# A scan layer on one core: the seam between the power levels and the state inputs reordered

## The chip, the cores and the metric

The kernel runs on one core of one Trainium2 chip. The metric is the device time of one execution in microseconds (us). Five engines run side by side, each with its own instruction queue, and order each other by semaphores: TensorE (PE), VectorE (DVE), ScalarE (ACT), GpSimd (POOL) and SyncE (SP), which issues most of the DMA transfers.

## The reference, cut to what matters

Input x is (1, 8192, 512) in f32. It is normalised and modulated, goes through a linear state-space layer with a dense 16x16 matrix A per channel, and then through a layer norm, a GELU, an output product and a small feed-forward block. The part around the change is the state-space layer:

```python
def step(h, x_t):
    h = jnp.einsum('dnm,bdm->bdn', A, h) + Bm[None] * x_t[..., None]
    y_t = jnp.einsum('dn,bdn->bd', Cm, h) + Dm * x_t
    return (h, y_t)
_, y = jax.lax.scan(step, h0, jnp.swapaxes(x, 0, 1))
```

## The kernel before, in words

Time is cut into 64 chunks of 128 steps (NC = 64, L = 128). Within a chunk the layer is a convolution with the taps C A^k B; between chunks a state of 16 numbers per channel is carried. The 512 channels are done in two halves of 32 groups of 8 channels (8 x 16 = 128 partitions). For each half the engines go through these stages:

- **Levels** (L1198, L1201): 28 steps (STEPS = 7 levels x OCT = 4 octets of 8 groups) double the number of known vectors A^k B (array PV) and of transposed ones (WP). In each step POOL lays out the power of A as block diagonals (L421), DVE transposes them (L847), PE multiplies, and ACT copies the results from PSUM (L638 to L640, semaphore lvl_ev). Step n of PE waits for the transposes of step n and for the copies of step n - 2. In half 0, ACT also normalises the columns of x between the steps (L579, semaphore xh_r), and DVE takes their statistics.
- **Column sums** (L905): when the last level of an octet is copied, DVE sums PV over time, one reduction for each of four octets. L942 makes from them the bias SB of the state inputs (sb_r).
- **Taps** (L1211): 64 matmuls of CM (C spread over groups, made by POOL at L454, cm_r) with PV give the convolution taps (semaphore k_mm). DVE takes them from PSUM (L951 to L956), and SP writes them to memory, from where they are later loaded as Toeplitz tiles.
- **State inputs**: for q = 0 to 7, PE transposes four groups of PV (L1220, `input_mats(q)`, ut_mm), ACT copies them to SBUF (L648, ut_ev), PE multiplies them with x (L1237, the input product, u_mm), ACT scales and biases the even channels and writes them into PV (L567, `even_inputs`), and DVE adds the odd ones (L967, u_ev). Product q waits for u_ev of q - 4.
- **Scan** (L1262) over the chunks, and then the **output products** (L1305, L1310) for 32 groups.

After both halves comes the feed-forward part, from 368 us to the end. Every engine's order is written out by hand in its queue; each instruction waits on semaphores, and whatever stands behind a waiting instruction on the same engine waits too. Two queues matter here. In DVE's, the reduction of octet o stood right behind the transposes (L847) of a step and ahead of those of the next step, in each of the last three steps. In PE's, the 64 tap matmuls stood behind the last level step and ahead of the first input transposes.

Of the kernel before, what the change touches and what calls it, by code (L numbers as in the profile page):

```python
# [12 lines left out]
P = 128  # L13
# [3 lines left out]
L = P  # L17
# [6 lines left out]
OCT = HG // 8  # L24
# [5 lines left out]
STEPS = LEVELS * OCT  # L30
SSTEPS = SCANS * OCT
HSTEPS = STEPS + SSTEPS
ESTEPS = HSTEPS - OCT
# [40 lines left out]
def adaln_ssm_kernel(nc, x_in, A_in, Bm_in, Cm_in, Dm_in, lnw_in, lnb_in, Wo_in, bo_in,  # L74
# [12 lines left out]
    with ctx:  # L87
# [55 lines left out]
        CM = UR.rearrange("p (g c) -> p g c", c=4 * GC)  # L143
# [407 lines left out]
        def _(act):  # L551
# [7 lines left out]
            def even_inputs(half, q):  # L559

                act.wait_ge(S["parca_r"], 2)
                act.wait_ge(S["sb_r"], half + 1)
                act.wait_ge(S["u_mm"], 8 * half + q + 1)
                ps = PS[:, q % 4, :].rearrange("p (g c a) -> p g a c", g=4, a=2)
                for i in range(4):
                    g = half * HG + 4 * q + i
                    ins = act.activation(PV[:, 4 * q + i, H0:H0 + NC], ps[:, i, 0, :], ACT.Identity, scale=parca[:, 0, g:g + 1],  # L567
                                         bias=SB[:, g:g + 1])
                ins.then_inc(S["ua_r"], 1)
# [196 lines left out]
        def _(dve):  # L766
# [134 lines left out]
            def column_sums(half, o):  # L901

                dve.wait_ge(S["lvl_ev"], half * ESTEPS + STEPS - OCT + o + 1)
                sums = SB[:, half * HG + 8 * o:half * HG + 8 * o + 8]
                dve.reduce_sum(sums, PV[:, 8 * o:8 * o + 8, 0:L], AX.X).then_inc(S["sums_r"], 1)  # L905

            for half in range(HALVES):
                base = half * HSTEPS
                for n in range(STEPS):
                    if half == 0 or n >= AHEAD:  # L910
                        power_mats(half, n)
                    if half == 0 and n == 0:
                        first_column(0)
                    if half == 0 and n == 6:
                        first_tap()
                    if half == 0:
                        for c in stats_of(n):
                            stats_x(c)
                        if n == MOD_A + 1:
                            mod_columns()  # L920
                        if n == MOD_B + 1:
                            gates()
                        if n == MOD_B + 2:
                            dve.wait_ge(S["col_ev"], 4)
                            dve.tensor_tensor(picked.rearrange("p (s j) -> p s j", j=NS), casa[:, :].unsqueeze(2).to_broadcast([P, 2 * QB, NS]),
                                              em[:, GC:].unsqueeze(1).to_broadcast([P, 2 * QB, NS]), ALU.mult).then_inc(S["pick_r"], 1)

                    if n > STEPS - OCT:
                        column_sums(half, n - 1 - (STEPS - OCT))
                    if half and 4 <= n < 4 + EARLY:  # L930
                        dve.wait_ge(S["y_ev"], HG)
                        dve.bn_stats(ebs[:, n - 4, 0, :], column(n - 4)[:, 0:HD // 2, :]).then_inc(S["ebs_r"], 1)

                column_sums(half, OCT - 1)
                if half == 0:
                    dve.wait_ge(S["cst_ev"], 1)
                    for a in range(2):
                        dve.tensor_scalar(parca[:, a, :], CST[:, 0:NG], par[:, a:a + 1], None, ALU.mult).then_inc(S["parca_r"], 1)
                dve.wait_ge(S["cst_ev"], 1)
                dve.wait_ge(S["sums_r"], OCT * (half + 1))  # L940
                sums = SB[:, half * HG:(half + 1) * HG]
                dve.tensor_tensor(sums, sums, CST[:, NG + half * HG:NG + (half + 1) * HG], ALU.mult).then_inc(S["sb_r"], 1)  # L942

                for i in range(OCT):
                    power_mats(half, STEPS + i)

                dve.wait_ge(S["k_mm"], half + 1)
                dve.wait_ge(S["kz_r"], half + 1)
                if half == 0:
                    dve.wait_ge(S["ld_small"], 48)  # L950
                chain(dve.tensor_copy(ktu, PS[:, 4, 0:HD].rearrange("p (b w) -> p b w", b=2)))  # L951
                chain(dve.tensor_copy(ktu[:, :, L - 1], DmT[:, 2 * half:2 * half + 2]))
                for b in range(2):
                    dve.tensor_scalar(ktz[:, b, 0:L], ktu[:, b, :], casa[:, 2 * half + b:2 * half + b + 1], None, ALU.mult).then_inc(S["kt_r"], 1)
                for b in range(2):
                    dve.tensor_scalar(ktsa[:, b, :], ktu[:, b, :], casa[:, QB + 2 * half + b:QB + 2 * half + b + 1], None,  # L956
                                      ALU.mult).then_inc(S["ksa_r"], 1)

                dve.wait_ge(S["parca_r"], 2)
                for q in range(8):  # L960
                    n = 8 * half + q
                    dve.wait_ge(S["ua_r"], n + 1)
                    ps = PS[:, q % 4, :].rearrange("p (g c a) -> p g a c", g=4, a=2)
                    for i in range(4):
                        g = half * HG + 4 * q + i
                        st = PV[:, 4 * q + i, H0:H0 + NC]
                        ins = dve.scalar_tensor_tensor(out=st, in0=ps[:, i, 1, :], scalar=parca[:, 1, g:g + 1], in1=st, op0=ALU.mult,  # L967
                                                       op1=ALU.add)
                    ins.then_inc(S["u_ev"], 1)
                dve.wait_ge(S["u_ev"], 8 * (half + 1))  # L970
                for i in range(SSTEPS):
                    k, o, n = i // OCT, i % OCT, base + STEPS + i
                    if OCT <= i + 2 < SSTEPS:
                        power_mats(half, STEPS + i + 2)

                    if i >= 1:
                        scan_add(dve, S, PV, scan_ps, half, base, i - 1, ALU)
                scan_add(dve, S, PV, scan_ps, half, base, SSTEPS - 1, ALU)
                for g in range(HG):
                    if half == 0 and g == HG - 12:  # L980
                        first_mix(1)
                    if half == 0 and g == HG - 8:
                        first_column(1)
                    if half == 0 and g == HG - 4:
                        for i in range(AHEAD):
                            power_mats(1, i)
                    if half == HALVES - 1 and g in (26, 27, 30, 31):
                        q = (26, 27, 30, 31).index(g)
                        dve.wait_ge(S["wo_tr"], q + 1)
                        if q >= 2:  # L990
                            dve.wait_ge(S["t_mm"], HG + 30)
                        dve.tensor_tensor(WoT[:, q, :], PS[:, 6 + q % 2, :], GA, ALU.mult).then_inc(S["wo_ev"], 1)
                    y_out(half * HG + g, g)
                    if half == HALVES - 1:
                        last_weights(g)
# [137 lines left out]
        def _(pe):  # L1133
# [41 lines left out]
            for half in range(HALVES):  # L1175
# [26 lines left out]
                                           start=True, stop=True)  # L1202
                    mm.then_inc(S["lvl_mm"], 1)

                pe.wait_ge(S["lvl_ev"], half * ESTEPS + STEPS)
                pe.wait_ge(S["cm_r"], 4 * (half + 1))
                for b in range(2):
                    for m in range(4):
                        for e in range(4):
                            g = (4 * b + e) * 4 + m  # L1210
                            mm = pe.matmul(PS[32 * e:32 * e + 32, 4, b * P:(b + 1) * P], CM[:, g, :], PV[:, g, 1:L + 1],  # L1211
                                           start=(m == 0), stop=(m == 3))
                mm.then_inc(S["k_mm"], 1)

                def input_mats(q):
                    n = 8 * half + q
# [5 lines left out]

                if half == 0:
                    pe.wait_ge(S["cst_ev"], 1)
                    pe.wait_ge(S["xh_r"], NC)
                input_mats(0)
                for q in range(8):
                    n = 8 * half + q
                    if q < 7:
                        input_mats(q + 1)  # L1230
                    pe.wait_ge(S["ut_ev"], n + 1)
                    if q >= 4:
# [1 line left out]
                    for i in range(4):  # L1234
                        for e in range(4):
# [2 lines left out]
                                           Uring[:, q % 2, i * P + 32 * e:i * P + 32 * e + 32], pair_of(d // 2),  # L1238
                                           start=True, stop=True)
                    mm.then_inc(S["u_mm"], 1)  # L1240
                    if q == 4:
                        pe.wait_ge(S["ksa_r"], 2 * (half + 1))
                        for b in range(2):
                            mm = pe.transpose(PS[:, 4, HD + b * P:HD + (b + 1) * P], ktsa[:, b, :], ident[:, :])
                        mm.then_inc(S["ktt_mm"], 1)
# [254 lines left out]
```

## Time and profile before

| what | us |
|---|---|
| median of 3 runs | 753.96 |
| the three runs | 755.10, 750.85, 753.96 |
| the profiled execution, its own time | 752.96 |
| its span in the profile | 751.0 |

The profile is of one execution; its times count from the start of the span. A row of the timeline gives the start, the length, the engine, the line of the kernel and the operation; in brackets stands how long the engine was idle before it and what released it. Rows of equal instructions are merged, so a length can stand for several of them.

### The profile page before, as it was taken

To read this page: it belongs to the slowest core of one execution; us is meant where nothing else is said; L and a number is where in the kernel's file an instruction comes from. 1 tells how busy PE (TensorE), PEld (TensorE's weight loads), DVE (VectorE), ACT (ScalarE), POOL (GpSimd) and SP (SyncE) were. 2 spreads that over 40 slices of the span, in tenths; PEclk is the share of its full clock that TensorE was granted. 3 is DMA by queue.
4 is the path that set the end of the run, shared out by engine and by line. 5 is a ranking of instruction groups with operands and counts; after the bars stand their busy time and mean duration, and the time that the engine had idled before them with its cause. 6 is when DMAs were issued, how large, how long until landed. Compare 5 with 4: busy or idle time off the path is not lost.

```text
span 751.0 us, 24826 instructions
## 1 busy us (share of the span) xinstructions
PE 703.9 (94%) x10079; PEld 491.7 (65%) x10079; DVE 524.6 (70%) x1193; ACT 501.2 (67%) x1079; POOL 467.1 (62%) x684
## 2 busy tenths in 40 slices
PE   5797889999999899999699999999999999999997
PEld 4776777887899879888445545555545555545563
DVE  7887956744643568447445888878888878887676
ACT  1586978834223488444346998888898888898872
POOL 5665632543355505643589887888888888887610
PEclk9999999999999999999799999999999999999999
DMA  7978400277400002598503012232322232221113
GB/s 225 357 227 298 157 17 4 49 162 162 102 4 4 3 24 46 130 197 185 196 0 113 2 57 94 83 105 85 101 95 99 85 101 112 78 92 56 58 49 149
DMA packets 78210, 78.18 MB, mean 104 GB/s; under 512 B 16144, under 2 KB 49552, under 8 KB 78096
## 3 DMA queue, kind: packets, MB, share of 16 engines
q1 hardware_dynamic: 77072, 74.76, 33.4%
q10 hardware_dynamic: 1024, 1.84, 0.9%
q8 instruction: 80, 1.31, 0.7%
q14 instruction: 34, 0.28, 0.1%
HBM read 59.28 MB, written 17.30 MB: 102 GB/s over the span
## 4 chain that ended last, share of the span: by engine, by line
PE 50%; DVE 1%; POOL 0%; ACT 0%; DVEq 0%; issue 0%; ACTq 0%; POOLq 0%
PE PS L1336 31%; PE PS L1405 5%; PE PS L1383 4%; PE PS L1328 4%; PE PS L1370 4%; PE PS L1420 1%; PE PS L1346 1%; PE PS L1357 0%; ACT arenaC L686 0%; DVE ebs L1005 0%; PE PS L1350 0%; DVE arenaC L1021 0%; DVEq L87 0%; POOL sy L399 0%; DVE XY L859 0%
## 5 line engine op out<-in xcount | busy, mean ns | idle before, releaser
L1336 PE MATMUL PS<-arenaC,arenaA 128*128 128x512 f32 x512 | 242.3, 606 | 0.0
L1336 PEld LDWEIGHTS PS<-arenaC,arenaA 128*128 128x128 f32 x512 | 90.3, 191 | 87.9 <-issue 83.4
L1198 PE MATMUL PS<-arenaA,arenaC 64*64 64x80 f32 (+1 forms) x1792 | 119.0, 235 | 7.7 <-DVE arenaC L847 3.7
L1201 PE MATMUL PS<-arenaA,arenaC 64*64 64x64 f32 (+1 forms) x1792 | 117.1, 221 | 3.6 <-issue 3.4
L722 ACT ACTIVATE arenaA<-PS,ffc 128x256 f32<-128x256 f32 x224 | 112.2, 581 | 12.3 <-PE PS L1383 12.3
L1051 DVE SCALAR_TENSOR_TENSOR PS<-arenaA,ffc,PS 128x256 f32<-128x256 f32 x196 | 95.2, 486 | 21.7 <-ACT arenaA L722 5.7
L1198 PEld LDWEIGHTS PS<-arenaA,arenaC 64*64 64x64 f32 x1792 | 99.5, 140 | 14.3 <-issue 6.1
L1201 PEld LDWEIGHTS PS<-arenaA,arenaC 64*64 64x64 f32 x1792 | 102.5, 139 | 4.0 <-issue 4.0
L694 ACT ACTIVATE arenaA<-PS,lnwb 128x256 f32<-128x256 f32 x128 | 65.9, 576 | 44.6 <-PE PS L1328 44.6
L421 POOL TENSOR_TENSOR arenaC<-arenaA,par 128x512 f32<-128x512 f32 x64 | 66.0, 1041 | 38.2 <-DVE arenaC L847 13.4
L519 POOL TENSOR_TENSOR ROWS<-ROWS 128x512 f32<-128x512 f32 x64 | 81.6, 1275 | 5.3
L859 DVE TENSOR_TENSOR XY<-PS,arenaA 128x256 f32<-128x256 f32 x128 | 48.3, 420 | 50.2 <-PE PS L1310 50.1
L675 ACT ACTIVATE arenaC<-arenaC 64x512 f32<-64x512 f32 x64 | 39.8, 629 | 63.0 <-DMA arenaC<-kernel_taps 62.8
L1310 PEld LDWEIGHTS PS<-XY,arenaC 128*64 128x64 f32 x2048 | 63.2, 136 | 12.0 <-ACT arenaC L675 7.0
L1310 PE MATMUL PS<-XY,arenaC 128*64 128x64 f32 x2048 | 67.6, 222 | 3.7 <-ACT arenaC L675 3.1
L847 DVE STREAM_TRANSPOSE arenaC<-arenaC 128x512 f32<-128x512 f32 x64 | 44.7, 703 | 33.5 <-POOL arenaC L421 26.6
L638 ACT ACTIVATE arenaA<-PS 128x128 f32<-128x128 f32 x56 | 15.6, 278 | 72.3 <-PE PS L1201 72.0
L483 POOL TENSOR_TENSOR arenaC<-arenaA,par 128x252 f32<-128x252 f32 x64 | 37.6, 619 | 39.9 <-PE PS L1305 39.8
L1262 PE MATMUL PS<-arenaA,arenaC 64*64 64x80 f32 (+1 forms) x1536 | 56.8, 229 | 2.3 <-DVE arenaA L967 1.2
L1328 PEld LDWEIGHTS PS<-ident,arenaC 128*128 128x128 f32 x256 | 32.6, 143 | 40.1 <-issue 40.1
L1262 PEld LDWEIGHTS PS<-arenaA,arenaC 64*64 64x64 f32 x1536 | 53.2, 133 | 6.3 <-ACT arenaC L668 4.0
L416 POOL TENSOR_TENSOR arenaC<-arenaA,par 128x256 f32<-128x256 f32 x40 | 24.5, 614 | 52.2 <-ACT arenaA L662 52.2
(202 smaller groups left out, 1352.0 us busy)
## 6 DMA issues: line engine op xcount, KB each, us to landing
arenaC<-kernel_taps SPq DMA_DIRECT2D x64, 256.0 KB, 5.1
XY<-in_L_attn_x SPq DMA_DIRECT2D x38, 256.0 KB, 5.6
arenaC<-in_L_attn_x SPq DMA_DIRECT2D x15, 512.0 KB, 3.7
out<-arenaC SPq DMA_DIRECT2D x15, 512.0 KB, 2.7
arenaC<-in_L_attn_x SPq DMA_DIRECT2D x26, 256.0 KB, 4.9
XY<-in_L_wmod SPq DMA_DIRECT2D x6, 1024.0 KB, 9.1
XY<-in_L_attn_x SPq DMA_DIRECT2D x11, 512.0 KB, 3.7
out<-XY SPq DMA_DIRECT2D x10, 512.0 KB, 2.8
```

The lines of the kernel that those rows point to most:

```text
L421: gp.tensor_tensor(BDs[:, step % BDR, :, :].rearrange("p g (a m) -> p g a m", m=NS), src, msk, ALU.mult).then_inc(S["bdp_r"], 1)
L519: chain(gp.tensor_tensor(tmp, tmp, Grow, ALU.mult))
L694: act.activation(zT[:, u % 2, q, :].rearrange("p (t i) -> p t i", i=P), PS[:, b, (q % 2) * UW:(q % 2 + 1) * UW].rearrange("p (t i) -> p t ...
L722: act.activation(rr[:, h % RELU_RING, :], PS[:, bank, 0:FP * P], ACT.Relu, scale=W1c[:, h:h + 1], bias=b1c[:, h:h + 1]).then_inc(S["relu_r ...
L859: ins = dve.tensor_tensor(dst, src, row, ALU.add)
L1051: ins = dve.scalar_tensor_tensor(out=dst, in0=rr[:, h % RELU_RING, :], scalar=W2c[:, h:h + 1], in1=g, op0=ALU.mult, op1=ALU.add)
L1198: pe.matmul(pv_ps(r)[e:e + BW, j, LW - nw:LW + NS], BDTs[e:e + BW, b, j, :], PV[e:e + BW, g, PW - nw:PW + NS], start=True, stop=True)
L1201: mm = pe.matmul(w_ps(r)[e:e + BW, j, LW - nw:LW], BDs[e:e + BW, b, j, :], WP[e:e + BW, g, L + 1 - nw:L + 1], start=True, stop=True)
L1262: mm = pe.matmul(scan_ps(i)[e:e + BW, j, 0:w], BDTs[e:e + BW, n % BDR, j, :], PV[e:e + BW, g, H0:H0 + w], start=True, stop=True)
L1310: mm = pe.matmul(PS[a:a + 64, t_bank(g), h * NC:(h + 1) * NC], Tring[g % TR][:, h, a:a + 64], channel(n * GC + h), start=False, stop=(h == ...
L1328: mm = pe.transpose(PS[:, b, i:i + P], hatY[:, t, q * P:(q + 1) * P], ident[:, :])
L1336: mm = pe.matmul(PS[:, 2 + t, :], zT[:, u % 2, q, t * P:(t + 1) * P], WoT[:, q, :], start=False, stop=(q == QB - 1))
```

## The change

The column sums of the first three octets move in DVE's queue behind all the transposes of the levels; the last one moves behind the two small L938 operations. PE transposes the first two groups of input matrices (q = 0 and 1) ahead of the taps. In half 1 the taps then follow at once, in two parts that wait for one octet's copies less and for the last; in half 0 the first input product comes ahead of the taps too. Because the even inputs overwrite columns of PV that the taps read, ACT's `even_inputs` now also waits for k_mm.

```diff
@@ ACT, even_inputs
                 act.wait_ge(S["u_mm"], 8 * half + q + 1)
+                act.wait_ge(S["k_mm"], half + 1)
@@ DVE, in and behind the loop over the steps
-                    if n > STEPS - OCT:
-                        column_sums(half, n - 1 - (STEPS - OCT))
...
-                column_sums(half, OCT - 1)
+                for o in range(OCT - 1):
+                    column_sums(half, o)
                 if half == 0:
                     dve.wait_ge(S["cst_ev"], 1)
                     for a in range(2):
                         dve.tensor_scalar(parca[:, a, :], CST[:, 0:NG], par[:, a:a + 1], None, ALU.mult).then_inc(S["parca_r"], 1)
+                column_sums(half, OCT - 1)
@@ PE, behind the last step
-                pe.wait_ge(S["lvl_ev"], half * ESTEPS + STEPS)
-                pe.wait_ge(S["cm_r"], 4 * (half + 1))
-                for b in range(2):
-                    for m in range(4):
...
-                mm.then_inc(S["k_mm"], 1)
+                def taps():
+
+                    pe.wait_ge(S["lvl_ev"], half * ESTEPS + STEPS - 1)
+                    pe.wait_ge(S["cm_r"], 4 * (half + 1))
+                    for b in range(2):
+                        if b:
+                            pe.wait_ge(S["lvl_ev"], half * ESTEPS + STEPS)
+                        for m in range(4):
+                            for e in range(4):
+                                g = (4 * b + e) * 4 + m
+                                mm = pe.matmul(PS[32 * e:32 * e + 32, 4, b * P:(b + 1) * P], CM[:, g, :], PV[:, g, 1:L + 1],
+                                               start=(m == 0), stop=(m == 3))
+                    mm.then_inc(S["k_mm"], 1)
...
                 if half == 0:
                     pe.wait_ge(S["cst_ev"], 1)
+                input_mats(0)
+                input_mats(1)
+                if half:
+                    taps()
+                else:
                     pe.wait_ge(S["xh_r"], NC)
-                input_mats(0)
                 for q in range(8):
                     n = 8 * half + q
-                    if q < 7:
+                    if 0 < q < 7:
                         input_mats(q + 1)
...
                     mm.then_inc(S["u_mm"], 1)
+                    if half == 0 and q == 0:
+                        taps()
```

## Rows read from the trace of the kernel before

**Rows 1.** The page, part 1: busy time of the engines over the span.

```profile
PE 703.9 (94%) x10079; PEld 491.7 (65%) x10079; DVE 524.6 (70%) x1193; ACT 501.2 (67%) x1079; POOL 467.1 (62%) x684
```

**Rows 2.** The page, part 4: the chain that ended last, by engine.

```profile
PE 50%; DVE 1%; POOL 0%; ACT 0%; DVEq 0%; issue 0%; ACTq 0%; POOLq 0%
```

**Rows 3.** PE's waits, 80 to 101 and 240 to 262 us.

```profile
PE PS L1198 <- DVE arenaC L847: 1.9, 1, 1.9
...
PE PS L1211 <- ACT arenaA L640: 1.4, 1, 1.4
```

**Rows 4.** Timeline of half 0's seam, in order of start; idle time in brackets.

```profile
92.36 1.22 DVE L905 TENSOR_REDUCE b1f<-arenaA 128x8 f32<-128x1024 f32 x1 [1.14 <-ACT arenaA L640]
93.49 0.70 DVE L847 STREAM_TRANSPOSE arenaC<-arenaC 128x512 f32<-128x512 f32 x1
...
94.25 0.35 PE L1198 MATMUL PS<-arenaA,arenaC 64*64 64x80 f32 x4 [1.85 <-DVE arenaC L847]
...
95.41 2.27 ACT L579 ACTIVATE XY<-arenaC,ST 128x512 f32<-128x512 f32 x3
...
98.12 0.28 ACT L638 ACTIVATE arenaA<-PS 128x128 f32<-128x128 f32 x1 [0.43 <-PE PS L1201]
...
101.29 0.63 ACT L640 ACTIVATE arenaA<-PS 128x512 f32<-128x512 f32 x1
101.93 1.10 POOL L454 TENSOR_TENSOR arenaC<-bcs,mask 128x64 f32<-128x64 f32 x4
101.95 1.22 DVE L905 TENSOR_REDUCE b1f<-arenaA 128x8 f32<-128x1024 f32 x1 [1.33 <-ACT arenaA L640]
...
103.17 1.96 PE L1211 MATMUL PS<-arenaA,arenaC 128*32 128x128 f32 x64 [3.03 <-POOL arenaC L454]
...
105.06 1.09 PE L1220 MATMUL PS<-ident,arenaA 128*128 128x128 f32 x8
...
105.75 1.09 ACT L648 ACTIVATE arenaC<-PS 128x512 f32<-128x512 f32 x2 [3.83 <-PE PS L1220]
...
106.40 1.08 PE L1237 MATMUL PS<-XY,arenaC 128*32 128x128 f32 x32 [0.25 <-ACT arenaC L648]
...
107.60 0.71 DVE L847 STREAM_TRANSPOSE arenaC<-arenaC 128x512 f32<-128x512 f32 x1 [0.29 <-POOL arenaC L421]
107.64 1.29 ACT L567 ACTIVATE arenaA<-PS,b1f 128x64 f32<-128x64 f32 x4 [0.79 <-PE PS L1237]
...
108.24 0.39 DVE L951 COPY arenaC<-PS 128x256 f32<-128x256 f32 x1
...
109.29 1.31 ACT L567 ACTIVATE arenaA<-PS,b1f 128x64 f32<-128x64 f32 x4
...
109.65 1.84 DVE L967 SCALAR_TENSOR_TENSOR arenaA<-PS,b1f,arenaA 128x64 f32<-128x64 f32 x8
...
112.81 1.08 PE L1237 MATMUL PS<-XY,arenaC 128*32 128x128 f32 x32
```

**Rows 5.** Timeline of half 1's seam, in order of start.

```profile
253.93 0.35 PE L1198 MATMUL PS<-arenaA,arenaC 64*64 64x80 f32 x4 [1.19 <-DVE arenaC L847]
...
258.92 0.61 ACT L640 ACTIVATE arenaA<-PS 128x512 f32<-128x512 f32 x1
...
259.58 1.96 PE L1211 MATMUL PS<-arenaA,arenaC 128*32 128x128 f32 x64 [1.36 <-ACT arenaA L640]
...
262.81 1.08 PE L1237 MATMUL PS<-XY,arenaC 128*32 128x128 f32 x32 [0.25 <-ACT arenaC L648]
...
264.04 1.29 ACT L567 ACTIVATE arenaA<-PS,b1f 128x64 f32<-128x64 f32 x4 [0.80 <-PE PS L1237]
```

**Rows 6.** Stretches of 1 us: busy time by engine, then PE's granted clock, DMA.

```profile
97.00:98.00 1.00, 1.00 (x22) 1.00 (x21) 0.45 (x1) 0.68 (x1) 0.00 (x0) 0.50 0.00 0
...
103.00:104.00 1.00, 0.82 (x32) 0.86 (x36) 0.60 (x4) 0.00 (x0) 1.00 (x3) 1.00 0.00 0
307.00:308.00 1.00, 1.00 (x8) 0.77 (x6) 0.00 (x0) 0.00 (x0) 0.56 (x2) 0.50 1.01 319
```

More of the change, by code:

```diff
@@ L1203, in _ @@
                     mm.then_inc(S["lvl_mm"], 1)
-                pe.wait_ge(S["lvl_ev"], half * ESTEPS + STEPS)
-                pe.wait_ge(S["cm_r"], 4 * (half + 1))
-                for b in range(2):
-                    for m in range(4):
[L1209 to L1212, printed above, removed]
-                mm.then_inc(S["k_mm"], 1)
+                def taps():
[10 more added lines that the diff above has]
+                    mm.then_inc(S["k_mm"], 1)
                 def input_mats(q):
```

## The prediction

> **What bounds the kernel now.** I read the busy times first: PE is busy for 94% of the span and no other engine for more than 70% [rows 1]. The chain that ended last is PE's for half of the span and hardly anyone else's [rows 2]. Followed back it reaches only to 368 us, where the feed-forward part begins, so it says nothing of the two halves before; there I went to the waits. The halves run one after the other, the second needs PV and the tap buffers that the first leaves, and the feed-forward part needs both. So a microsecond taken out of the seam of a half is worth a microsecond at the end, unless something later in that half goes by a clock of its own.
>
> PE's waits around the two seams name the two things that the edit touches: a level step that waits for DVE's transposes, and the taps, that wait for ACT's copies [rows 3]. The timeline shows why. In half 0 the reduction of octet 0 starts at 92.36, as soon as the copies it reads are there, and the transposes for the next step stand behind it and start at 93.49; PE begins at 94.25 after 1.85 us of idleness [rows 4]. In half 1 the same place costs PE 1.19 us [rows 5]. At the end of the levels ACT finishes its copies in half 0 at 101.29 + 0.63 = 101.92, then has nothing to do for 3.83 us: PE waits until 103.17 for CM, does the taps, and only then the transposes that ACT copies at 105.75. The first input product starts at 106.40, the first even input at 107.64 [rows 4]. In half 1 copies end at 258.92 + 0.61 = 259.53, and the first even input is at 264.04 [rows 5]. From there on ACT sets the pace: the even inputs of q = 0 and 1 start 109.29 - 107.64 = 1.65 us apart, with the 1.3 us of the inputs and the next copy filling that time [rows 4]. So the start of the first even input is the quantity to follow, and I take what it moves as what the half gains.
>
> **The change part by part.** No instruction and no DMA is added; only the order and the waits change. So each term is a wait.
>
> *Column sums, half 0.* Without the reduction ahead of them the transposes of step 26 are done before ACT ends its copies, and PE saves up to 1.85 us. But ACT is at that time busy with normalising, from 95.41 to 97.68, and takes the step's result at 98.12, 0.43 us after it came free [rows 4]. Only this 0.43 us reaches the end of the levels. I take 0.4, bounds 0 and 0.43.
>
> *Column sums, half 1.* Here ACT has no normalising; PE's 1.19 us [rows 5] go through in full. I take 1.2, bounds 0.8 and 1.33 (the idle row counts from the end of the last matmul, and back to back steps overlap by a tenth).
>
> *The sums themselves, later.* They are needed for sb_r, ahead of the first even input. Three reductions of 1.22 us run while the last steps are copied, and the last starts, as before, when the last copy ends: 101.95 and 1.22 us [rows 4], so SB is there about 1.4 us behind the copies. The first even input comes 2.9 us behind them in half 1 and 3.85 in half 0 (below). The cost is nothing; the cover is 1.5 us and 2.4.
>
> *Half 0, the reorder.* The eight transposes (1.09 us) go into the time in which PE waited 3.03 us. ACT copies them at once behind its own last copy, without the 3.83 us of idleness. From the first copy to the product it is 106.40 - 105.75 = 0.65, the product takes 1.08, the taps 1.96, and from a product's end to the even input 107.64 - 107.48 = 0.16 [rows 4]. The even input waits now for the taps, so it comes 0.65 + 1.08 + 1.96 + 0.16 = 3.85 us behind the end of the copies, against 107.64 - 101.92 = 5.72: 1.9 us earlier. CM was ready at 101.93 + 1.10 = 103.03 [rows 4] and POOL waits for ACT's last normalising, which comes 0.4 earlier; the product ends at 101.92 + 0.65 + 1.08 = 103.65 on the old scale, so the taps do not wait for CM.
>
> *The added wait for k_mm.* Behind it on ACT stand the even inputs and the copy of q = 2. The copy of q = 1 stands ahead, so PE can go on with the transposes of q = 2 and product 1 behind the taps; that is the old distance between first product and first even input. Nothing else is queued there.
>
> *DVE behind it, half 0.* DVE takes the taps at 108.24, when its transposes from 107.60 are done, and those wait for POOL, not for the taps [rows 4]. This moves by 0.4 only, so the odd inputs start at 109.25 instead of 109.65, while the first even ones are ready at 105.3 + 1.3 = 106.6. The backlog is 2.6 us, and DVE takes 1.84 / 2 = 0.92 us for each q against 1.65 on ACT [rows 4], so it has caught up at the fourth or fifth. Product 4 waits for the first odd input: 110.2 against a start of 112.81 - 2.3 = 110.5. It fits by 0.3 us. The SP queue, which stores the taps, moves with DVE: 0.4.
>
> *Half 1, the reorder.* PE's last step ended at 259.58 - 1.36 = 258.22. The transposes and the taps follow without a gap, 258.22 + 1.09 + 1.96 = 261.27, since the second part of the taps needs the copies of 259.53 only at 260.3. The product starts at 261.27 against 262.81 [rows 5]: 1.5 us, and 1.7 with the overlap of back to back groups. I take 1.6.
>
> *Sum.* Half 0: 0.4 + 1.9 = 2.3. Half 1: 1.2 + 1.6 = 2.8. Together 5.1 us. The profiled execution's span of 751.0 becomes 745.9 and its own time of 752.96 becomes 747.9. It lies 1.0 under the median shown; from the median of 753.96 I get 748.9, and I forecast that.
>
> *The clock.* In the new order PE has an empty stretch in half 0. Its last step starts when ACT's copies of the step two before are done (95.4) and takes half of 258.22 - 253.93, 2.1 us; with the transposes PE is out of work at about 98.7 and begins the product at about 102.1, some 3.4 us later. The rows don't decide what the clock does: after 1.85 us of idleness at 94.25 PE's clock was granted at 0.50, that is 1.2 GHz, in the row of 97 us, and after 3.03 us it stayed at 1.00 in the row of 103 us [rows 4, 6]. It was also at 0.50 at 307 us with PE busy throughout [rows 6]. The Trainium skill (TensorE: Matmul & The Clock Gate, "Why this matters for your kernels") warns against idle gaps between bursts of matmuls because the clock falls back to half. By that rule the first product and the taps would run at half rate, and the sum would be as in the first rival. The trace agrees at 94 us and does not at 103 us.
>
> **The rivals.**
>
> *The clock falls in half 0's gap.* Product and taps are 1.08 + 1.96 = 3.0 us of work. If all of it ran at half rate it would cost 3.0; in the stretch around 97 us the low clock ended with PE at work, so I price it at half, 1.6. Then the total is 5.1 - 1.6 = 3.5, and 750.5 us.
>
> *Half 0 gains nothing.* If DVE doesn't catch up, product 4 and with it the rest wait for DVE, which hangs on POOL. The margin of 0.3 us speaks for it, the 0.92 against 1.65 against it. Then half 1 alone counts with the 0.4: 3.2, 750.8 us.
>
> *Nothing reaches the end.* The scan or the output products could go by something that does not start with the state inputs, such as the tap loads. Against it: the scan needs every state input, and the store of the taps runs long before. 754.0 us.
>
> *Slower.* The low clock of the gap would have to hold through all eight input products. At half rate PE would need about 3.2 us for each q instead of 1.65, eight times 1.5 makes 12, less 5.1: 761 us. It decides once the clock stays low for more than some 10 us of PE's work, since at half rate every 2 us lose 1 and 5.1 are to be lost. Against it: the stretch at 97 us ended under load.
>
> **How the numbers follow.** Forecast 0.61; clock 0.15; half 0 without gain 0.10; nothing 0.08; slower 0.04; more than 6.3 us gained 0.02. The forecast's own range is 747.6 to 750.2. For 8 in 10 I take in the clock's and half 0's cases above, and below the upper bounds of the terms (5.6 us) and a low stretch like that of 307 us that falls away, with the runs shown lying 4.3 us apart: 745.8 to 751.8. What a measurement can tell from no change is 0.5%, 3.8 us. The forecast lies over it by 1.3, so nine tenths of its chance, a third of the clock's and the last case are faster by more: 0.62. Nothing, half 0 without gain and the rest are within: 0.34. Slower 0.04.
>
> **What would show it.** Right: L905 for octets 0 to 2 in a row behind the last L847 of the levels; no idleness of PE from L847 in front of step 26; L648 directly behind the last L640 in both halves; first L567 about 2.3 us earlier in half 0 and 5.1 us earlier in half 1; L1262 earlier by the same. Wrong: a granted clock of 0.50 over product 0 and taps, an idle PE in front of product 4 released by L967, or a first L1305 that hasn't moved.

## The result, and the profile after

The changed kernel took 748.37 us in the median of seven runs (745.43 to 749.43), the kernel before 753.96 (750.85 to 755.10, also seven runs): a ratio of 0.9929, 95% interval 0.9904 to 0.9953. That is 5.6 us less, against 5.1 forecast. The single profiled executions stand at spans of 747.5 and 751.0 us, 3.5 us apart.

The page of the changed kernel, parts 1 and 4, answers to [rows 1, 2]. All lines behind the added wait are one higher: L640 is L641, L567 is L568; on PE, L1211 is L1216, L1220 is L1225, L1237 is L1246.

```profile
PE 700.9 (94%) x10079; PEld 490.1 (66%) x10079; DVE 524.6 (70%) x1193; ACT 501.2 (67%) x1079; POOL 467.1 (62%) x684
...
PE 50%; DVE 1%; POOL 0%; ACT 0%; DVEq 0%; issue 0%; ACTq 0%; POOLq 0%
```

The counts of working instructions are the same on every engine. The timeline of half 0's seam, in order of start, answers to [rows 4]:

```profile
92.53 0.36 PE L1199 MATMUL PS<-arenaA,arenaC 64*64 64x80 f32 x4 [0.28 <-ACT arenaA L641]
...
95.09 2.30 DVE L906 TENSOR_REDUCE b1f<-arenaA 128x8 f32<-128x1024 f32 x2
...
97.59 0.36 ACT L639 ACTIVATE arenaA<-PS 128x128 f32<-128x128 f32 x1
...
97.99 1.09 PE L1225 MATMUL PS<-ident,arenaA 128*128 128x128 f32 x8
...
100.75 0.73 ACT L641 ACTIVATE arenaA<-PS 128x512 f32<-128x512 f32 x1
101.23 1.22 ACT L649 ACTIVATE arenaC<-PS 128x512 f32<-128x512 f32 x2
...
102.10 1.93 PE L1246 MATMUL PS<-XY,arenaC 128*32 128x128 f32 x32 [3.02 <-ACT arenaC L649]
103.78 3.67 PE L1216 MATMUL PS<-arenaA,arenaC 128*32 128x128 f32 x64
107.59 1.29 ACT L568 ACTIVATE arenaA<-PS,b1f 128x64 f32<-128x64 f32 x4 [5.14 <-PE PS L1216]
...
109.19 0.85 DVE L968 SCALAR_TENSOR_TENSOR arenaA<-PS,b1f,arenaA 128x64 f32<-128x64 f32 x4
109.44 1.29 ACT L568 ACTIVATE arenaA<-PS,b1f 128x64 f32<-128x64 f32 x4
```

The order is the planned one. The idle 1.85 us before step 26 are 0.28, ACT takes the step's result at 97.59 without the 0.43 of waiting, the two copies follow directly on the last one, and the product starts at 102.10, as worked out. But product and taps take 1.93 and 3.67 us instead of 1.08 and 1.96, and the first even input comes at 107.59, 6.11 us behind the last copy (100.75 + 0.73 = 101.48); before it was 5.72. The granted clock (the number behind POOL's busy time) says why:

```profile
101.00:102.00 1.00, 0.00 (x0) 0.00 (x0) 0.49 (x1) 1.00 (x3) 0.92 (x3) 0.50 0.00 0
103.00:104.00 1.00, 1.00 (x25) 1.00 (x21) 0.02 (x1) 0.00 (x0) 1.00 (x3) 0.50 0.06 16
106.00:107.00 1.00, 1.00 (x25) 0.99 (x20) 0.71 (x1) 0.00 (x0) 1.00 (x2) 0.50 0.00 0
307.00:308.00 1.00, 1.00 (x39) 0.93 (x34) 0.76 (x2) 0.26 (x1) 0.32 (x1) 1.00 0.91 208
```

The clock fell to 0.50, 1.2 GHz, in the 3.02 us in which PE had nothing to do, and came back only after 107. That is the sign of being wrong that the prediction names, 0.50 over product 0 and taps, and half 0's first even input is only 0.05 us earlier than before (107.59 against 107.64) in place of the 2.3 forecast.

The row of 307 us, 0.50 in [rows 6], stands at 1.00 here. The low stretch there lay over the first output products of half 1, and they were the longer for it, by 3.64 - 2.43 = 1.2 us from their start to the start of the next group. Before:

```profile
306.22 3.71 PE L1305 MATMUL PS<-arenaC,arenaA 64*128 64x256 f32 x16 [0.52 <-DVE arenaA L1475]
309.86 2.33 PE L1310 MATMUL PS<-XY,arenaC 128*64 128x64 f32 x72
```

and after, where L1305 is L1316:

```profile
301.61 0.70 PE L1316 MATMUL PS<-arenaC,arenaA 64*128 64x256 f32 x4 [0.53 <-DVE arenaA L1486]
302.54 1.57 PE L1316 MATMUL PS<-arenaC,arenaA 64*128 64x256 f32 x12 [0.23 <-POOL arenaC L483]
304.04 2.18 PE L1321 MATMUL PS<-XY,arenaC 128*64 128x64 f32 x65
```

Half 1's seam answers to [rows 5]:

```profile
255.30 1.09 PE L1225 MATMUL PS<-ident,arenaA 128*128 128x128 f32 x8
256.06 0.61 ACT L641 ACTIVATE arenaA<-PS 128x512 f32<-128x512 f32 x1
256.32 1.96 PE L1216 MATMUL PS<-arenaA,arenaC 128*32 128x128 f32 x64
256.54 1.10 ACT L649 ACTIVATE arenaC<-PS 128x512 f32<-128x512 f32 x2
...
258.02 0.19 DVE L943 TENSOR_TENSOR b1f<-b1f,bcs 128x32 f32<-128x32 f32 x1
258.10 1.06 PE L1246 MATMUL PS<-XY,arenaC 128*32 128x128 f32 x32
...
259.36 1.29 ACT L568 ACTIVATE arenaA<-PS,b1f 128x64 f32<-128x64 f32 x4 [1.71 <-PE PS L1246]
```

PE goes from transposes to taps to product with no idle row among them; the first even input is 2.69 us behind the last copy, before 4.51. The levels of half 1 are shorter too. The last copy of octet 0 is, before,

```profile
251.40 0.61 ACT L640 ACTIVATE arenaA<-PS 128x512 f32<-128x512 f32 x1
```

and after,

```profile
249.94 0.61 ACT L641 ACTIVATE arenaA<-PS 128x512 f32<-128x512 f32 x1
```

and those of octet 3 start at 258.92 [rows 5] and 256.06: 7.52 us apart before, 6.12 after.

Half 1's first even input is 4.68 us earlier than before, against 5.1 forecast, but 1.4 us of that lie in half 0's output products, which the change does not touch.

So in this pair of traces half 0's seam gave nothing and half 1's seam and levels gave it all, and yet the medians are further apart than forecast. What half 0 is worth was the question for the runs.

### The profile page after: what moved, and what is told of

Read it like the earlier page. It is cut to its first block, busy times and chain, and to the rows that moved or that the text cites. A ratio compares the mean times of both kernels' runs of the same rounds, so it can differ in the third digit from the quotient of the medians.

```text
span 747.5 us, 24842 instructions
## 1 busy us (share of the span) xinstructions
PE 700.9 (94%) x10079; PEld 490.1 (66%) x10079; DVE 524.6 (70%) x1193; ACT 501.2 (67%) x1079; POOL 467.1 (62%) x684
## 4 chain that ended last, share of the span: by engine, by line
PE 50%; DVE 1%; POOL 0%; ACT 0%; DVEq 0%; issue 0%; ACTq 0%; POOLq 0%
PE PS L1347 31%; PE PS L1416 5%; PE PS L1394 4%; PE PS L1339 4%; PE PS L1381 4%; PE PS L1431 1%; PE PS L1357 1%; PE PS L1368 0%; ACT arenaC L687 0%; DVE ebs L1006 0%; DVE arenaC L1022 0%; PE PS L1361 0%; DVEq L87 0%; POOL sy L399 0%; DVE XY L860 0%
## 5 line engine op out<-in xcount | busy, mean ns | idle before, releaser
L1199 PE MATMUL PS<-arenaA,arenaC 64*64 64x80 f32 (+1 forms) x1792 | 115.5, 232 | 6.2 <-issue 2.6
L723 ACT ACTIVATE arenaA<-PS,ffc 128x256 f32<-128x256 f32 x224 | 111.9, 578 | 12.3 <-PE PS L1394 12.3
L1202 PE MATMUL PS<-arenaA,arenaC 64*64 64x64 f32 (+1 forms) x1792 | 114.1, 217 | 4.8 <-issue 4.8
L1199 PEld LDWEIGHTS PS<-arenaA,arenaC 64*64 64x64 f32 x1792 | 102.1, 137 | 12.7 <-issue 7.2
L1202 PEld LDWEIGHTS PS<-arenaA,arenaC 64*64 64x64 f32 x1792 | 104.5, 136 | 5.4 <-issue 5.4
L1273 PE MATMUL PS<-arenaA,arenaC 64*64 64x80 f32 (+1 forms) x1536 | 56.9, 229 | 2.3 <-DVE arenaA L968 1.3
L1273 PEld LDWEIGHTS PS<-arenaA,arenaC 64*64 64x64 f32 x1536 | 53.3, 133 | 6.4 <-ACT arenaC L669 3.9
```

The lines of the kernel that those rows point to most:

```text
L723: act.activation(rr[:, h % RELU_RING, :], PS[:, bank, 0:FP * P], ACT.Relu, scale=W1c[:, h:h + 1], bias=b1c[:, h:h + 1]).then_inc(S["relu_r ...
L1199: pe.matmul(pv_ps(r)[e:e + BW, j, LW - nw:LW + NS], BDTs[e:e + BW, b, j, :], PV[e:e + BW, g, PW - nw:PW + NS], start=True, stop=True)
L1202: mm = pe.matmul(w_ps(r)[e:e + BW, j, LW - nw:LW], BDs[e:e + BW, b, j, :], WP[e:e + BW, g, L + 1 - nw:L + 1], start=True, stop=True)
L1273: mm = pe.matmul(scan_ps(i)[e:e + BW, j, 0:w], BDTs[e:e + BW, n % BDR, j, :], PV[e:e + BW, g, H0:H0 + w], start=True, stop=True)
```

## The experiments

All runs of one group shared a chip and its runs of the kernel before, whose medians were 753.25, 752.64 and 753.32 us in the three groups. The first group has the changed kernel again, the column sums alone, the changed kernel without half 0's order and the one filled with six; the second has the one filled with three, the old sums in half 0, half 0's order alone and the second trace of the kernel before; the third has half 1's order alone and the repeats of the changed kernel, of the one filled with three and of the old sums in half 0. The ratio to the kernel before is the recorded one; it is not the quotient of the two medians and differs from it by up to 0.0018. Three figures carry the comparison; they are read from each run's timeline as in the section above: from the last copy of the levels (end of the last L640 or L641) to the first even input (start of the first L567 or L568), in half 0 and in half 1; and between them the levels of half 1, from the end of half 0's last output product to the last copy of half 1.

| kernel | half 0: copy to even input | PE idle ahead of taps or first product | clock over them | levels of half 1 | half 1: copy to even input |
|---|---|---|---|---|---|
| before | 5.72 | 3.03 | up | 56.98 | 4.51 |
| before, second trace | 6.96 | 2.88 | fell | 56.73 | 4.51 |
| half 1's order alone | 7.02 | 3.08 | fell | 57.39 | 2.67 |
| half 0's order alone | 3.60 | 1.24 | up | 56.51 | 4.57 |
| column sums alone | 7.85 | 4.66 | fell | 55.19 | 4.51 |
| changed, without half 0's order | 7.92 | 4.66 | fell | 55.11 | 2.68 |
| changed | 6.11 | 3.02 | fell | 55.27 | 2.69 |
| changed, second trace | 6.11 | 3.01 | fell | 55.65 | 2.67 |
| changed, third trace | 3.59 | 3.01 | up | 55.41 | 2.68 |
| changed, filled with six | 5.84 | none | up | 55.13 | 2.69 |
| changed, filled with three | 3.60 | 0.28 | up | 55.11 | 2.68 |
| changed, filled with three, second trace | 3.60 | 0.27 | up | 55.11 | 2.68 |
| changed, old sums in half 0 | 3.59 | 1.24 | up | 55.10 | 2.68 |
| changed, old sums in half 0, second trace | 3.59 | 1.35 | up | 55.10 | 2.68 |

**The changed kernel again.** No edit.

> The changed kernel once more, as the measure for the other three on the same chip. Both theories: ratio to before near 0.993. The theory that the clock falls in half 0's gap in every execution expects a granted clock of 0.50 over the first input product and the taps of half 0 here as well, and the first even input of half 0 at about 107.6 us; the rival, that the profiled execution was one of few, expects 1.00 there and about 105.2 us.

748.25 us, ratio 0.9924 (0.9897 to 0.9951); the clock fell again. On its own this speaks for the theory that it always falls. A repeat in the third group contradicts it:

> The changed kernel, as the measure for the next two on the same chip: half 0's last copy to the first even input 6.1 us with a granted clock of 0.50, half 1's 2.7 us.

746.73 us, ratio 0.9918 (0.9881 to 0.9954), and in its trace the clock did not fall. The third trace's timeline:

```profile
99.51 0.70 ACT L641 ACTIVATE arenaA<-PS 128x512 f32<-128x512 f32 x1
...
100.83 1.08 PE L1246 MATMUL PS<-XY,arenaC 128*32 128x128 f32 x32 [3.01 <-ACT arenaC L649]
101.70 1.96 PE L1216 MATMUL PS<-arenaA,arenaC 128*32 128x128 f32 x64
...
103.80 1.29 ACT L568 ACTIVATE arenaA<-PS,b1f 128x64 f32<-128x64 f32 x4 [2.62 <-PE PS L1216]
```

and the stretch with the granted clock:

```profile
101.00:102.00 1.00, 1.00 (x44) 1.00 (x40) 0.65 (x2) 0.17 (x1) 1.00 (x4) 1.00 0.00 0
```

The same kernel, the same idle 3.01 us: here 1.08 and 1.96 us, and 103.80 - 100.21 = 3.59 to the even input. The price of the fall is 6.11 - 3.59 = 2.5 us. (The way on to the scan is another 0.2 longer in the two traces with the fall, 12.3 us against 12.1.)

**Column sums alone.**

```diff
-                    if n > STEPS - OCT:
-                        column_sums(half, n - 1 - (STEPS - OCT))
...
+                for o in range(OCT - 1):
+                    column_sums(half, o)
...
+                column_sums(half, OCT - 1)
```

> The column sums' part of the change alone; PE's order and the waits as before. By the waits in the trace: 0.4 us in half 0 and 1.2 in half 1, together 1.6 us faster (ratio 0.998), and no idleness of PE ahead of step 26 from the transposes. Rival, the reductions were hidden and the sums' move only shifts work: 0, with the first taps of half 1 at the same distance from the end of step 25 as before.

752.61 us, ratio 0.9981 (0.9957 to 1.0005): the ratio expected, but not told from nothing. The trace shows two effects that work against each other. Half 1's levels are shorter (55.19 against 56.98 and 56.73). In half 0, PE's steps end earlier, but the taps still wait for CM:

```profile
103.17 3.64 PE L1211 MATMUL PS<-arenaA,arenaC 128*32 128x128 f32 x64 [4.66 <-POOL arenaC L454]
106.75 1.83 PE L1220 MATMUL PS<-ident,arenaA 128*128 128x128 f32 x8
```

and the stretch with the granted clock:

```profile
104.00:105.00 1.00, 1.00 (x27) 1.00 (x23) 0.41 (x1) 0.00 (x0) 1.00 (x2) 0.50 0.09 16
```

PE's waiting grew from 3.03 to 4.66 us, the clock fell, and taps and transposes ran at half rate: 7.85 us instead of 5.72.

**The changed kernel without half 0's order.** PE's old order in half 0, the rest as changed; the diff is against the changed kernel.

```diff
-                input_mats(0)
-                input_mats(1)
                 if half:
+                    input_mats(0)
+                    input_mats(1)
                     taps()
                 else:
+                    taps()
                     pe.wait_ge(S["xh_r"], NC)
+                    input_mats(0)
...
-                    if half == 0 and q == 0:
-                        taps()
```

> The changed kernel with the old order of PE in half 0 (taps, then transposes, then products); column sums and half 1 as in the changed one. Clock theory: half 0's reorder is worth 0 to 0.3 us, so the time is that of the changed kernel (ratio to before 0.993, the same within 0.1%). Rival, the fall was one execution's: 1.9 us slower than the changed kernel (0.9955).

750.87 us, ratio 0.9975 (0.9948 to 1.0002), 2.6 us over the changed kernel of the same group. That lies nearer to the rival, but not for the rival's reason, since the clock is down in this trace. The clock theory as put there is wrong: half 0's order is worth 7.92 - 6.11 = 1.8 us at the seam with the clock down, too, since the sums alone have brought it down already. The seam shows this; the two intervals of the totals overlap.

**Half 1's order alone.** PE's order of half 1, with the sums and half 0's order as before (the diff is against the kernel before, whose taps stood ahead of this; a `taps()` is the same 64 matmuls, in the two parts of the changed kernel, which in half 0 still wait for CM, and the even inputs have the added wait for k_mm).

```diff
...
+                if half:
+                    input_mats(0)
+                    input_mats(1)
+                    taps()
+                else:
+                    taps()
                     pe.wait_ge(S["xh_r"], NC)
-                input_mats(0)
+                    input_mats(0)
...
```

> PE's new order in half 1 alone, sums and half 0 as before. By the stages: half 1's last copy to the first even input 2.7 us instead of 4.5, everything else as before, so 1.8 us faster (ratio to before 0.9976). Rival, the gain needs the sums out of the way: SB comes too late behind the last reduction and the distance stays above 3 us.

752.24 us, ratio 0.9986 (0.9956 to 1.0017): the total tells neither the 1.8 us expected nor nothing. Half 1's seam is 2.67 as expected, so the sums are not in its way. Half 0 has the old order and the old sums here, and the clock fell (7.02).

**Half 0's order alone.** Sums and half 1 as before; the diff is against the changed kernel, which has the sums moved besides.

```diff
...
-                input_mats(0)
-                input_mats(1)
                 if half:
+                    pe.wait_ge(S["lvl_ev"], half * ESTEPS + STEPS)
                     taps()
+                    input_mats(0)
                 else:
+                    input_mats(0)
+                    input_mats(1)
                     pe.wait_ge(S["xh_r"], NC)
...
```

> PE's new order in half 0 alone; column sums and half 1 as before. Clock theory: the clock stays up in half 0 and the first even input comes 3.9 us behind the last copy instead of 5.7, so 1.8 us faster than before (ratio 0.9976). Rival, the new order's gap brings the clock down by itself: about 6 us, 0.4 us slower than before.

751.71 us, ratio 0.9994 (0.9966 to 1.0021): the total doesn't show it. The trace does, 3.60 us with the clock at 1.00, for with the sums in their old place PE ends its steps late and is idle for 1.24 us only:

```profile
102.41 1.08 PE L1248 MATMUL PS<-XY,arenaC 128*32 128x128 f32 x32 [1.24 <-ACT arenaC L649]
103.28 1.96 PE L1216 MATMUL PS<-arenaA,arenaC 128*32 128x128 f32 x64
```

and the stretch with the granted clock:

```profile
103.00:104.00 1.00, 1.00 (x48) 1.00 (x40) 0.46 (x4) 0.00 (x0) 1.00 (x2) 1.00 0.00 0
```

**The kernel before, a second trace.** No edit.

> The kernel before once more, for a second trace of it: how far the stages that the change does not touch differ from one execution to the next. Expected: 5.7 us from half 0's last copy to the first even input and 4.5 us in half 1, as in the first trace; the output products of each half differing by a microsecond or two, as they do between the traces so far (51.4 to 52.7 and 54.1 to 56.2 us). If half 0's seam is 7 us or more here, the clock falls in the old order too, and half 0's gain is larger than the one pair of traces shows.

756.34 us in its one run, with 748.01 to 756.97 in the 29 runs of its group. The old order loses the clock as well:

```profile
103.84 2.52 PE L1211 MATMUL PS<-arenaA,arenaC 128*32 128x128 f32 x64 [2.88 <-POOL arenaC L454]
106.29 1.97 PE L1220 MATMUL PS<-ident,arenaA 128*128 128x128 f32 x8
```

and the stretch with the granted clock:

```profile
106.00:107.00 1.00, 1.00 (x12) 0.71 (x5) 0.71 (x1) 0.00 (x0) 1.00 (x2) 0.50 0.00 0
```

That is 6.96 us, and with half 1's order alone, which has the same half 0, 7.02. The trace that the prediction rests on was the good case of three.

**The gap filled.** Matmuls into a part of PSUM that the taps overwrite; nothing reads their result. Six at first, then three.

```diff
                 else:
+                    pe.wait_ge(S["lvl_ev"], STEPS - 1)
+                    for i in range(3):
+                        pe.matmul(PS[:, 4, :], ident[:, :], PV[:, 0:4, 0:L], start=True, stop=True)
                     pe.wait_ge(S["xh_r"], NC)
```

> The changed kernel with six matmuls of 128x512 more in half 0's gap, which write a part of PSUM that the taps overwrite; their result is not used. Clock theory: the clock stays at 1.00, the first even input of half 0 comes at about 105.2 us instead of 107.6, and the kernel is about 2.3 us faster than the changed one (ratio to before 0.990). Rival, half 0's reorder gains nothing for another reason (DVE or the transfers behind it): the clock stays up, but the scan of half 0 does not start earlier than 119.9 us, and the time is that of the changed kernel (0.993). If the filler itself is too long, the first product starts later than 102.1 us.

With six, 749.53 us, ratio 0.9952 (0.9931 to 0.9973), no faster than the changed kernel of its group (748.25). The clock stayed up, but the filler was too long: each f32 matmul of 512 columns stands as two in the trace, and the product waited behind them.

```profile
101.82 5.42 PE L1237 MATMUL PS<-arenaA,ident 128*128 128x512 f32 x12
...
104.08 1.19 ACT L649 ACTIVATE arenaC<-PS 128x512 f32<-128x512 f32 x2
...
107.16 1.08 PE L1249 MATMUL PS<-XY,arenaC 128*32 128x128 f32 x32
108.06 1.93 PE L1216 MATMUL PS<-arenaA,arenaC 128*32 128x128 f32 x64
```

> The changed kernel with three matmuls of 128x512 (2.7 us by the 0.45 us of each of the twelve passes seen before) in half 0's gap; their result is not used. Clock theory: granted clock 1.00 over the first input product and the taps, the first even input 3.85 us behind the last copy instead of 6.1, and the kernel 2.2 us faster than the changed one (ratio to before 0.990). Rival, the clock falls all the same or something else holds the even input: still about 6 us, time as the changed kernel (0.993).

With three, 746.04 us, ratio 0.9918 (0.9892 to 0.9944), and 3.60 us at the seam:

```profile
100.59 2.84 PE L1237 MATMUL PS<-arenaA,ident 128*128 128x512 f32 x6
...
103.71 1.08 PE L1249 MATMUL PS<-XY,arenaC 128*32 128x128 f32 x32 [0.28 <-ACT arenaC L649]
104.58 1.96 PE L1216 MATMUL PS<-arenaA,arenaC 128*32 128x128 f32 x64
```

> The changed kernel with three filling matmuls, against the changed kernel on the same chip: 6.1 - 3.6 = 2.5 us faster if the clock falls in most executions of the changed kernel; the same if the two traces in which it fell were chance.

Beside the changed kernel: 745.77 against 746.73 us (0.9897, 0.9858 to 0.9936, against 0.9918). The expected 2.5 us don't show, and the intervals are too wide to rule them out; the changed kernel's own trace of this group had the clock up. The seam is shown, a faster total is not.

**Old sums in half 0, all else as changed.**

```diff
+                    if half == 0 and n > STEPS - OCT:
+                        column_sums(half, n - 1 - (STEPS - OCT))
...
-                for o in range(OCT - 1):
+                for o in range(OCT - 1) if half else ():
```

> The changed kernel with the column sums in their old place in half 0 and in the new one in half 1. Clock theory: PE's last level step ends later, at about 100.1 us, so PE's gap ahead of the first product shrinks to about 1.3 us, the clock stays up, and the first even input comes about 3.9 us behind the last copy instead of 6.1; the sums' move costs 0.4 at the end of the levels, so 1.8 us faster than the changed kernel (ratio 0.9905). Rival, the sums' move in half 0 helps as predicted: 0.4 us slower than the changed kernel.

> The changed kernel with the column sums of half 0 in their old place, against the changed kernel on the same chip: 2.5 us less by the clock and 0.4 more by the end of the levels, 2.1 us faster; the same or 0.4 slower if the fall was chance.

746.72 us (0.9939, 0.9910 to 0.9968), and beside the changed kernel 747.63 (0.9927, 0.9896 to 0.9958). The seam is 3.59 both times, idle 1.24 and 1.35 us with the clock up; the total can't be told from that of the changed kernel (746.73 beside the second).

The first of the two traces shows one thing more. Ahead of step 26 PE is idle for 1.85 us, exactly as in the kernel before, but here the clock stays up:

```profile
95.36 0.36 PE L1201 MATMUL PS<-arenaA,arenaC 64*64 64x80 f32 x4 [1.85 <-DVE arenaC L848]
96.51 2.29 ACT L580 ACTIVATE XY<-arenaC,ST 128x512 f32<-128x512 f32 x3
98.63 0.33 ACT L639 ACTIVATE arenaA<-PS 128x128 f32<-128x128 f32 x1
```

ACT goes from normalising to the step's result without a wait. In the kernel before it waited 0.43 us at this place [rows 4], with the step run at 0.50. It is so in all six traces with the old sums in half 0: where the clock fell at this step (the kernel before, half 1's order alone, the second trace here) ACT waited 0.35 to 0.43 us, and from octet 0's last copy to octet 3's it is 9.54 to 9.60 us; where it stayed up (the other three) ACT didn't wait, and it is 9.05 to 9.06, as in the eight traces with the sums moved (9.06 to 9.08).

No version is shown to beat the changed one. Between executions of one kernel the total varies by more than the 2.5 us in question (the changed kernel in the first group: 742.97 to 752.73). The clock is a part of that: over the 88 executions of the kernel before in the three groups the time goes with the time at low clock, an estimate from each one's granted clock and time, 2 x (1 - clock) x time (correlation 0.66, 0.35 us for each us). That low time is also in line with the seams. In the mean over a kernel's executions it is 24 us with the sums alone and without half 0's order, where PE's wait is longest, 20 in the kernel before, 19 in the changed one, 17 with three filling matmuls and 15 with six. The output products are another part: from the first to the last of half 0's it is 51.2 to 53.7 us, of half 1's 53.5 to 56.2, and 1.2 to 1.4 us of this is the clock in four halves; and the levels of half 0 end anywhere from 100.2 to 104.3.

## Why the prediction was right

**The total.** 748.37 against 748.9, and the direction. It came from the seams named, but half 0's share came differently than summed, and the close fit is in part luck.

**Column sums, half 1.** Forecast 1.2, bound 1.33. From octet 0's last copy to octet 3's it is 7.53 us in all four traces with the old sums and 6.12 in all ten with the new: 1.4. The mechanism is right, the term mis-sized by 0.2. The whole levels of half 1 differ by 1.7 between the means (56.9 and 55.2); the other 0.3 lies ahead of octet 0's last copy, where the traces differ by up to 0.9 us with the sums in either place.

**Half 1, the reorder.** Forecast 1.6, measured 4.51 - 2.69 = 1.8, with or without the sums' move. That is the overlap of back to back groups that the prediction gave as 1.7.

**Column sums, half 0.** Forecast 0.4. The wait of ACT that the term rests on was there, but it came of the clock: by the six traces above, PE's hole ahead of step 26 costs 0.5 us when the clock falls at it and nothing when it doesn't, since ACT is normalising meanwhile. Over the three traces of the old order with the old sums the mean is 9.40, over those of the changed kernel 9.07: 0.3. In the old order of PE, which the prediction didn't need, the move also lengthens PE's wait ahead of the taps (3.03 to 4.66).

**Half 0, the reorder.** 3.85 us was forecast from last copy to first even input, and 3.59 or 3.60 was measured in each of the six traces with the clock up and no overlong filler: 5.72 - 3.59 = 2.1 us with the clock up in both, against 1.9. Most of the 0.25 too much is the overlap of back to back groups, since the taps start 0.87 us behind the product's start in the third trace, and the sum counts 1.08. Everything around it held: CM did not delay the taps, SB was in time, DVE had caught up before product 4 (in the third trace of the changed kernel the way from first even input to scan is 12.09 us, as before 12.10).

**The clock** is the step that failed, and in both kernels. The prediction gave the fall a chance of 0.15 and priced it at 1.6 us; it fell in two of three traces of the changed kernel and cost 2.5. But it took the seam of the kernel before as one in which the clock stays up, from one trace; in two more of its half 0 the clock fell, too, at a cost of 1.2 to 1.3. The means over three traces each are (5.72 + 6.96 + 7.02) / 3 = 6.6 and (6.11 + 6.11 + 3.59) / 3 = 5.3: half 0's seam is worth about 1.3 us in place of 1.9. Three traces each are few, and one fall more or less moves a mean by 0.4 to 0.8. With 0.3 for half 0's levels and 1.4 and 1.8 in half 1 that makes 4.8 in place of 5.1: half 0 gains 0.7 less than summed, half 1 gains 0.4 more.

A fourth part stands in no term of the sum. The low stretch over the first output products came in four of the six halves with both the old order and the old sums (from the first L1305 to the first L1310 3.6 to 3.8 us) and in none of the other 22 (2.4). As an estimate, four sixths of 1.2 us in each of two halves add 1.6 us to what the change gains. The prediction knew the stretch as one that might fall away and put it into the range only. Why the change should take it away is not shown. With it the parts make 6.4. The three pairs measured 5.6, 5.0 and 6.6 us between the medians, each give or take 2 to 3 by its interval, so the totals can't tell 4.8 from 6.4. That the forecast lies within 0.5 us of the first of them is luck, since its errors went both ways.

What decides whether the clock falls in a given execution is open. Idle times of 1.2 to 1.4 us ahead of product or taps kept it in three traces of three, 2.9 to 3.1 us lost it in four of six, 4.7 us lost it in two of two. But the 1.9 to 2.5 us ahead of step 26 lost it in three of six, and in the four falls over the first output products PE's longest idle time in the 8 us before was 0.52 us, so the length of a hole is not the whole of it. The Trainium skill (TensorE: Matmul & The Clock Gate, "Why this matters for your kernels") advises against idle gaps between bursts of matmuls; in the seams these traces agree, with the reservation that the same gap of the same kernel is harmless in one execution and costs 2.5 us in the next.

**The other rivals.** Half 0 without gain by a late DVE, no effect at the end, and a low clock through all input products did not occur: DVE was in time, the totals of all three pairs are lower with the whole interval, and in the changed kernel's first trace the clock is back by 108, and from the second product on everything runs at the old pace.

## What to carry to other kernels

Work that is moved out of a wait on TensorE leaves a longer hole behind it, and a hole can cost the clock of what follows; ask of every reorder how long the engine is empty ahead of the next burst, not only when that burst starts. Take the length of such a seam between two events of a neighbouring engine, over several traces: with the same order and the same clock it repeated to 0.1 us or better where the total varied by 10. And a clock state that one trace of the old kernel shows is a sample, not its rule: a wait read beside it can be the clock's doing and not that of the queue.

## What was not expected of the hardware

The clock stayed at 0.50 after PE had begun again with dense work: in the changed kernel's first trace product and taps ran at half rate from 102.1 to past 107. In the second trace of the kernel before it fell only more than a microsecond after the taps had begun (1.00 in the row of 103 us, with the taps starting at 103.84, and 0.50 in that of 106), so the clock can fall on work that seems safely behind an idle stretch; that this stretch brought it down is likely, not shown. An f32 matmul of 512 columns shows as two records, together 0.9 us (six in 5.42 us).
